# Softmax attention of one block regrouped from single heads to pairs of heads on half tiles of TensorE

## The reference, cut to what matters

```
q, k, v = split(x @ in_w.T + in_b)          # each 625 x 768, head h has 64 of the 768 columns
P  = softmax(q_h @ k_h.T / sqrt(64))         # 625 x 625 per head, rows sum to 1
o_h = P @ v_h                                # 625 x 64
x  = x + concat(o_h) @ out_w.T + out_b
```

## Time and profile before

| | us |
|---|---|
| median of 3 runs | 3425.65 (3424.79 to 3428.42) |
| the profiled execution, its own time | 3428.96 |
| its span | 3427.2 |
| PE busy | 2853.0 (83%) |
| DVE busy | 1476.2 (43%) |
| ACT busy | 1027.9 (30%) |
| POOL busy | 739.0 (22%) |
| the stage of the change, first score to last low part | 2333.98 to 2553.64 |

### The profile page before, as it was taken

The page is one execution under the profiler, slowest core; times in us unless marked ns, Lnnn a source line. Parts: engine busy times, 40 slices in busy tenths (PEclk is TensorE's granted clock), DMA queues, the critical chain, the costliest instruction groups (busy, mean ns, idle before and its releaser), DMA issues. The chain is left out here.

```text
span 3427.2 us, 47626 instructions
## 1 busy us (share of the span) xinstructions
PE 2853.0 (83%) x19703; PEld 2574.4 (75%) x19703; DVE 1476.2 (43%) x3577; ACT 1027.9 (30%) x1901; POOL 739.0 (22%) x314
## 2 busy tenths in 40 slices
PE   8788989996669898968779899799987779799587
PEld 7688978994339778968669799796566777596487
DVE  8944255653130225448434422415754541303633
ACT  0122235540012113239222333123442232255121
POOL 2422221110014112230225233230003231012222
PEclk9999999997889999979889899898998889899799
DMA  2022120006962102220112122121001221100011
GB/s 63 1 62 64 59 88 30 27 15 240 414 263 65 39 24 64 67 64 1 56 42 65 47 76 78 59 70 32 1 1 42 70 60 42 31 28 29 19 56 60
DMA packets 158969, 224.19 MB, mean 65 GB/s; under 512 B 16969, under 2 KB 136451, under 8 KB 158754
## 3 DMA queue, kind: packets, MB, share of 16 engines
q1 hardware_dynamic: 158754, 221.15, 19.6%
HBM read 219.20 MB, written 1.92 MB: 65 GB/s over the span
## 5 line engine op out<-in xcount | busy, mean ns | idle before, releaser
L47 PE MATMUL ps<-weights_r,buf_r 128*125 128x256 f32 (+2 forms) x4000 | 545.4, 290 | 43.0 <-DVE buf_r L2593 15.0
L47 PEld LDWEIGHTS ps<-weights_r,buf_r 128*125 128x125 f32 (+1 forms) x4000 | 519.2, 190 | 46.7 <-issue 40.1
L250 POOL TENSOR_TENSOR weights_r<-weights,weights_r 128x1536 fp32r<-128x1536 f32 (+1 forms) x79 | 270.0, 3418 | 1171.3 <-ACT weights_r L243 1171.3
L250 POOL TENSOR_TENSOR weights_r<-weights,head_weights_r 128x1536 fp32r<-128x1536 f32 (+1 forms) x78 | 270.1, 3463 | 1111.9 <-ACT head_weights_r L243 1111.9
L47 PE MATMUL ps<-xT_r,weights_r 128*128 128x376 f32 (+1 forms) x2100 | 345.8, 310 | 0.0
L47 PE MATMUL ps<-head_weights_r,buf_r 128*125 128x256 f32 (+1 forms) x2330 | 323.9, 285 | 0.0
L47 PEld LDWEIGHTS ps<-xT_r,weights_r 128*128 128x128 f32 x2100 | 314.9, 189 | 3.9 <-issue 1.1
L47 PEld LDWEIGHTS ps<-head_weights_r,buf_r 128*125 128x125 f32 x2330 | 300.3, 188 | 0.0
L824 PE MATMUL ps<-ident,buf 125*128 125x125 f32 x645 | 114.0, 351 | 179.6 <-DVE buf L899 98.6
L47 PE MATMUL ps<-weights_r,xT_r 128*125 128x256 f32 x1650 | 232.3, 285 | 26.1 <-DVE buf_r L688 8.7
L824 PEld LDWEIGHTS ps<-ident,buf 125*128 125x128 f32 x645 | 101.6, 188 | 192.2 <-issue 160.5
(11 more groups left out here) (297 smaller groups left out, 4405.2 us busy)
## 6 DMA issues: line engine op xcount, KB each, us to landing
expert_regions<-in_L_ffn_w SPq DMA_DIRECT2D x64, 576.0 KB, 15.2
expert_regions<-in_L_ffn_w SPq DMA_DIRECT2D x48, 768.0 KB, 15.8
weights<-in_L_mix_fc_w SPq DMA_DIRECT2D x24, 768.0 KB, 4.5
weights<-in_L_gnn_W SPq DMA_DIRECT2D x18, 768.0 KB, 4.6
weights<-in_L_ffn_W SPq DMA_DIRECT2D x12, 768.0 KB, 4.7
weights<-in_L_mix_w_mapT SPq DMA_DIRECT2D x9, 768.0 KB, 4.5
weights<-in_L_gnn_W_out SPq DMA_DIRECT2D x9, 768.0 KB, 4.7
weights<-in_L_mix_kqv_wT SPq DMA_DIRECT2D x9, 768.0 KB, 4.7
```

Of the source, the lines that this page charges most:

```text
L47: mm = net.nc.tensor.matmul(ps, net.r(stationary(s, k)), net.r(moving(m, k)), start=(n == 0 and k == 0), stop=(n == 2 and k == kc - 1))
L250: self.nc.gpsimd.tensor_tensor(self.r(load.dst), load.dst, self.r(load.high), ALU.subtract).then_inc(self.low_made, 1)
```

## The change

`SoftmaxPairs` takes the place of `SoftmaxHeads`. A step now handles a chunk c, that is two heads h = 0 and 1, in a different order:

- All 20 turn groups of the pair come first (j = 0 for both heads, then j = 1); ACT and DVE copy every other one. Each head has a buffer for P and one for turned P; P is no longer doubled across steps.
- The scores of the next pair come tile by tile, heads alternating: partitions 0 to 63, then 64 to 127. The largest score and its negation take one DVE instruction fewer (`top` and `neg` are one); `exp` no longer sums; `norm` is gone.
- Between the score tiles stand four pieces of the application: `out` for j = 0, `sum` for j = 0, `out` for j = 1, `sum` for j = 1. Each has 10 matmuls with 64 stationary columns: the value columns of head h, or 64 columns of ones, with the result on PSUM partitions 64h to 64h + 63 (`tile_position=(0, 64 * h)`), heads alternating.
- `inv` is the reciprocal of the sums, 128 partitions by 375 or 250 columns; `mul` writes out times inv to k's place; `hi` (ACT) and `low` (DVE) split it in two parts. inv, mul for j = 0 stand behind DVE's work on tile 2; those for j = 1 ahead of DVE's turn copies of the next step.

The core of the diff:

```diff
-class SoftmaxHeads(Heads):
+class SoftmaxPairs(Heads):
...
     def step(...)
...
-        for t in range(NT + 1):
-            if scores and t < NT:
-                pe += [("score", n, t, j) for j in range(2)]
-                dve += [("max", n, t, j) for j in range(2)] + [("top", n, t), ("neg", n, t)]
-            if apply and t < NT:
-                pe += [("turn", k, t, j) for j in range(2)]
-                act.append(("turn", k, t, 0))
-                dve.append(("turn", k, t, 1))
-            if scores and t < NT:
-                act += [("exp", n, t, j) for j in range(2)]
-            if scores and t > 0:
-                dve += [("sum", n, t - 1), ("rinv", n, t - 1), ("norm", n, t - 1)]
+        n = c + 1
         if apply:
-            for j in range(2):
-                pe.append(("apply", k, j))
-                act.append(("out", k, j))
-                dve.append(("out", k, j))
+            turns = [("turn", c, h, s, j) for j in range(2) for h in range(2) for s in range(NT)]
+            pe += turns
+            own = {e: [q for q in turns if self.turn_engine(*q[2:]) == e] for e in ("act", "dve")}
+            act += own["act"][:3] + ([("hi", c - 1, 1)] if c > 0 else []) + own["act"][3:]
+            dve += ([("inv", c - 1, 1), ("mul", c - 1, 1)] if c > 0 else []) + own["dve"] + ([("low", c - 1, 1)] if c > 0 else [])
+        pieces = [("apply", c, j, what) for j in range(2) for what in ("out", "sum")] if apply else []
+        for t in range(NT):
+            if scores:
+                pe += [("score", n, t, h, j) for j in range(2) for h in range(2)]
+                for h in range(2):
+                    dve += [("max", n, t, h, 0), ("max", n, t, h, 1), ("neg", n, t, h)]
+                    act += [("exp", n, t, h, 0), ("exp", n, t, h, 1)]
+            if t > 0 or not scores:
+                pe += pieces[:1]
+                pieces = pieces[1:]
+            if apply and t == 2:
+                dve += [("inv", c, 0), ("mul", c, 0)]
+            if apply and t == 3:
+                act += [("hi", c, 0)]
+        if apply:
+            dve += [("low", c, 0)]
...
     def reader(self, q):
         if q[0] == "score":
             return "act", ("exp",) + q[1:]
...
-        return "dve", ("out",) + q[1:]
+        return "dve", ("mul",) + q[1:3]
...
                 for s in range(NT):
-                    mm = nc.tensor.matmul(self.ps(q, 128, (t1 - t0) * TP), v[:, s, :], self.PT[:, s, t0 * TP:t1 * TP], start=(s == 0), stop=(s == NT - 1))
+                    for h in range(2):
+                        stationary = self.v[:, s, c * 128 + 64 * h:c * 128 + 64 * h + 64] if what == "out" else self.net.ones[:TP, 0:64]
+                        mm = nc.tensor.matmul(self.net.ps[64 * h:64 * h + 64, self.bank[q] % BANKS, 0:w], stationary, self.PT[h][:, s, ts],
+                                              start=(s == 0), stop=(s == NT - 1), tile_position=(0, 64 * h))
...
+                ins = nc.vector.reciprocal(self.inv[:, 0:w], self.ps(("apply", c, j, "sum"), 128, w))
...
+                ins = nc.vector.tensor_tensor(self.kT[:, c, ts], self.ps(("apply", c, j, "out"), 128, w), self.inv[:, 0:w], ALU.mult)
...
-    SoftmaxHeads(net, [(q, k, tok(G[2])[:, :, h // 2 * 128:(h // 2 + 1) * 128], halves[h % 2], Pair(q, k)) for h, (q, k) in enumerate(parts)],
-                 [feat(b, NT, TP) for b in (G[3], net.P1)], feat(G[4], NT, TP), 0.125)
+    SoftmaxPairs(net, feat(G[0]), feat(G[1]), tok(G[2]), [feat(b, NT, TP) for b in (G[3], net.P1)], [feat(b, NT, TP) for b in (G[4], net.XT)], net.fn, 0.125)
```

More of the change, by code:

```diff
@@ new lines, in __init__, with turn_engine, step @@
+        self.qT, self.kT, self.v, self.P, self.PT, self.inv, self.scale = qT, kT, v, P, PT, inv, scale
+        self.mx = net.st[:TP, 200:220].rearrange("p (t h j) -> p t h j", t=NT, h=2)
+        self.nb = net.st[:TP, 220:230].rearrange("p (t h) -> p t h", t=NT)
+        self.schedule(v.shape[2] // 128, -1, None)
+    def turn_engine(self, h, s, j):
+        return "act" if (s + h) % 2 == 0 else "dve"
+    def step(self, c, scores, apply):
+        pe, act, dve = (self.order[e] for e in ("pe", "act", "dve"))
+        n = c + 1
+        if apply:
+            turns = [("turn", c, h, s, j) for j in range(2) for h in range(2) for s in range(NT)]
[19 more added lines that the diff above has]
+            dve += [("low", c, 0)]
+        if apply and not scores:
+            dve += [("inv", c, 1), ("mul", c, 1), ("low", c, 1)]
+            act += [("hi", c, 1)]
@@ L1438, in tensor @@
             self.wait_bank(pe, q)
-            k = q[1]
-            qT, kT, v, half, out = self.heads[k]
+            c = q[1]
             if q[0] == "score":
-                t0, t1 = HALVES[q[3]]
-                mm = nc.tensor.matmul(self.ps(q, TP, (t1 - t0) * TP), qT[:, q[2] * TP:(q[2] + 1) * TP], kT[:, t0 * TP:t1 * TP], start=True, stop=True)
+                t, h, j = q[2:]
+                rows = slice(64 * h, 64 * h + 64)
+                ts, w = self.half(j)
+                mm = nc.tensor.matmul(self.ps(q, TP, w), self.qT[rows, c, t * TP:(t + 1) * TP], self.kT[rows, c, ts], start=True, stop=True)
@@ L1444, in tensor @@
             elif q[0] == "turn":
-                if q[2] == 0:
-                    self.wait(pe, "dve", "norm", k, HALVES[q[3]][1] - 1)
-                mm = self.turn_group(self.P[k % 2], q[2], *HALVES[q[3]], q)
-            else:
-                t0, t1 = HALVES[q[2]]
-                self.wait(pe, "act", "turn", k, NT - 1, 0)
-                self.wait(pe, "dve", "turn", k, NT - 1, 1)
+                h, s, j = q[2:]
+                if s == 0:
+                    self.wait(pe, "act", "exp", c, HALVES[j][1] - 1, h, 1)
@@ L1452, in tensor @@
+                mm = self.turn_group(self.P[h], s, *HALVES[j], q)
+            else:
+                j, what = q[2:]
+                ts, w = self.half(j)
+                if what == "out":
+                    for h in range(2):
+                        for s in range(NT):
+                            self.wait(pe, self.turn_engine(h, s, j), "turn", c, h, s, j)
                 for s in range(NT):
-                    mm = nc.tensor.matmul(self.ps(q, 128, (t1 - t0) * TP), v[:, s, :], self.PT[:, s, t0 * TP:t1 * TP], start=(s == 0), stop=(s == NT - 1))
+                    for h in range(2):
+                        stationary = self.v[:, s, c * 128 + 64 * h:c * 128 + 64 * h + 64] if what == "out" else self.net.ones[:TP, 0:64]
+                        mm = nc.tensor.matmul(self.net.ps[64 * h:64 * h + 64, self.bank[q] % BANKS, 0:w], stationary, self.PT[h][:, s, ts],
+                                              start=(s == 0), stop=(s == NT - 1), tile_position=(0, 64 * h))
@@ L1454, in tensor @@
             mm.then_inc(done.sem, done.one())
[L1456 to L1461, removed]
     def scalar(self, act):
@@ L1466, in scalar @@
         for q in self.order["act"]:
-            k, j = q[1], q[-1]
-            t0, t1 = HALVES[j]
+            c, j = q[1], q[-1]
+            ts, w = self.half(j)
             if q[0] == "turn":
+                h, s = q[2:4]
                 self.wait(act, "pe", *q)
[L1471 to L1475, removed]
-            else:
[L1477 to L1480, removed]
+                ins = nc.scalar.activation(self.PT[h][:, s, ts], self.ps(q, TP, w), ACT.Identity)
+            elif q[0] == "hi":
+                self.wait(act, "dve", "mul", c, j)
+                ins = nc.scalar.activation(self.net.r(self.qT[:, c, ts]), self.kT[:, c, ts], ACT.Identity)
+            else:
+                t, h = q[2:4]
+                self.wait(act, "dve", "neg", c, t, h)
+                if t == 0 and h == 0 and j == 0 and c > 0:
+                    self.wait(act, "pe", "turn", c - 1, 1, NT - 1, 1)
+                ins = nc.scalar.activation(self.P[h][:, t, ts], self.ps(("score", c, t, h, j), TP, w), ACT.Exp, bias=self.nb[:, t, h:h + 1], scale=self.scale)
             ins.then_inc(done.sem, done.one())
```

67 lines of the change are left out of this document (30 added, 37 removed).

## The result

The changed kernel takes 3373.68 us (median of 4 runs, 3370.6 to 3374.39), against 3426.42 for the kernel before in the same comparison (3424.79 to 3428.42). The ratio is 0.9844 with a 95% interval of 0.9827 to 0.9861: 1.6% faster, 52.7 us. The profiled execution took 3373.8 us, its span is 3371.9.

The account below looks back on a forecast made before the run. PE was taken as the bound, busy 155.5 of 171.7 us. Start 21, half-clock scores 2.8 and piece 2.7, five pairs of 28.6 and end 14.7 gave a 184.2 us stage, 35.5 less: median 3390, range 3378 to 3413.

Parts of the forecast that it names:

- the two stalls: PE waits for `mul` in each pair: about 2.4 us in tile 3, about 1.6 before the third turn group.
- The sum: Stage time added from its parts: 21 + 2.8 + 2.7 + 5 x 28.6 + 14.7 = 184.2 us, against 219.7.
- I take half clock: Start of the stage: the first turns, next scores and 5.5 us of the first piece run at half clock.
- T = 0: The moment PE is through with the turns; for the first pair forecast at 21 us into the stage.
- A steady pair: Two heads in the steady part of the stage: 28.6 us instead of 34.3.
- Scores: A score tile of both heads on different row halves: 1.4 us, between 1.11 (full overlap) and 2.20 (none).
- End: Last copy, four pieces with nothing between, then inv, mul, hi and low for 250 columns: 14.7 us.
- All stages behind start on `now()`, so it passes to the end: After the stage: its 35.5 us gain carries over to the whole kernel's time.
- The sums come free: Application: all four pieces take 11.0 us, as much as the two heads' applications before, row sums included.
- Rival 1: Row halves don't overlap: score tiles take 2.2 us, stage 204.3 us, time 3410; chance 0.15.
- Rival 2: Each PE change of kind costs 0.6 us instead of 0.15, losing 22 us of gain: 3412; chance 0.10.
- Rival 3: Clock falls in every pair at the stall before the third turn group, 10.6 us each: 3443; chance 0.05.

Follow-up runs that it names:

- experiment 1: The kernel before with ten extra fp32 matmuls ahead of the first two turn groups of the first head: 3417.02 us against 3427.63, ratio 0.9971.
- experiment 4: The changed kernel with one wait more, the first pair's turn groups waiting for the last exp of the first scores: 3382.3 us.
- experiment 5: The changed kernel with both heads' scores read from the first head's 64 partitions, so all on one row half: 3406.77 us.
- experiment 6: The changed kernel with the four score matmuls of a tile ordered by head instead of alternating: 3379.91 us.
- experiment 3: The changed kernel profiled again without any edit, also called the second profile: 3376.11 us.
- experiment 7: The changed kernel with each application piece's ten matmuls ordered by head, five of head 0, then five of head 1: 3412.9 us.

## Why the prediction was wrong

The direction and most of the mechanism were right: the overlap on both kinds of halves, the two stalls with their sizes, and the price of the reciprocals came as forecast. The time fell 4.3 us below the range, for two reasons. The sum had half clock at the start, which did not come, and the prediction let the gain of the stage pass to the end one for one, while 5.5 us more came behind the stage. With the stage's own miss alone, 11.4 us, the time would have been 3379, just inside the range.

- *The step that failed is "I take half clock" at the start.* Forecast: T = 0 at 21 us, with 2.6 us of it for half clock, and 2.8 and 2.7 us more for scores and the first piece at half clock, 8.1 in all. Measured: T = 0 at 16.5 us, clock 1.00, no half clock in the scores and the piece behind; in the second profile 17.1 us, with a fall of the clock that costs some 0.7. So 8.1 of the 11.4 us that the stage is short of 184.2 are this term. I argued that scores and turns at half clock had not brought the clock back before, and so would not now. But in the kernel before it fell at two holes of 3.19 and 2.31 us (experiment 1: fill them, and nothing falls). The new order's longest wait there is 1.76 us, since its turns need only ACT's exps, not DVE's chain of sum, reciprocal and scaling. Behind this wait the clock falls in some profiles, and behind a hole of 3.24 us it does so again (experiment 4), but it is back within a few us. I had this case as the lower bound of my own range, without asking what had made the clock fall.
- *The rest of the start*, 1.9 us: without half clock I had T = 0 at 18.4. The twenty exps take 2343.80 - 2334.71 = 9.1 us instead of 10.4, the copies behind them 4.1 instead of 4.4, and PE is through 0.3 us before the last copy ends:

```profile
2334.71 0.93 ACT L1497 ACTIVATE buf<-ps,stats 125x375 f32<-125x375 f32 x2
...
2343.80 1.23 ACT L1488 ACTIVATE buf<-ps 125x375 f32<-125x375 f32 x3
```

- *A steady pair*, forecast 28.6: 27.6 without a fall of the clock, 28.5 on the mean, so five pairs take 142.3 against 143. That the mean agrees so well is luck: the scores were priced 1.0 us too high, and the falls of the clock, which the sum did not have, cost 0.9. In the second profile, with one fall, the mean is 27.9. The parts: pieces 3.3 us, reciprocals 2.51 and 1.72, stalls 2.37 and 1.43, forecast 3.3, 2.50 and 1.72, 2.4 and 1.6.
- *Scores*, forecast 1.4 us for a tile and 0.15 for the change on either side: 1.25 with the change. The bound of full overlap (1.11 and a change) was the value; experiments 5 and 6 show the overlap, and that four matmuls are enough for it. This is the 1.0 us by which the undisturbed pair is shorter.
- *End*, forecast 14.7: 14.04.
- *Not in the sum*: the stages behind. "All stages behind start on `now()`, so it passes to the end" took their time as fixed. It was 5.6 us shorter in the first profile and 5.5 in the second, by the clock (experiment 3). No step of the prediction had it, and a profile of before alone does not give it. Why the clock is low for 17 us less there stays open. The 2.8 us ahead of the stage are no part of the result: the stage starts later in the second profile than in either of the kernel before.
- "The sums come free" holds only against the kernel before: all four pieces take what the two heads' applications took, but half of the pieces' columns are the sums', so a pair pays some 5.5 us of PE for them.
- Rival 1 is refuted by experiment 5. Rival 2 is refuted by the rows of the changed kernel: the changes of kind are in the 1.25 us. Rival 3 was right that a stall can lower the clock in a pair, and wrong in the place and the price: it falls at the stall in tile 3, in one or three of five pairs, for a few us, and costs 1.6 us where it does, not 10.6.

## What to carry to other kernels

Small matmuls on two halves of the array, rows or columns, ran here at the price of one, also in fp32, where the other half's work stood within four matmul records. So two half-width products with their row sums by columns of ones cost no more than two full-width products of which half was thrown away. When work is reordered, look for the wait that a stretch of low clock came from, and ask whether the new order still has it, before pricing the new work at that clock. Where a slow instruction (a wide reciprocal) needs only one of two products, make that product first and let the other cover it: this gave another 25 to 27 us on top of the change.

## What the runs showed of the hardware that was not expected

- Matmul records on different column halves do not start in the order of the program: in experiment 7 the 11th starts 0.31 us before the 8th.
- Ten matmuls of no use made the kernel before 0.29% faster (3427.63 to 3417.02 us), with the clock at 2.4 GHz through the whole stage, where it had been at 1.2 GHz for over 20 us.
- The same program behind the stage took 867.9 to 873.6 us in eleven profiles, with the granted clock low for a different number of us; an edit's effect of under 6 us on this kernel can be this alone.
- The clock fell behind a wait of some 1.7 us at the start in five of the seven profiles that have it, and was back while PE did nothing but scores.
